# A feed-forward up projection by seven block products in place of eight, on one Trainium2 core

## The chip, the cores and the metric

The kernel runs on one core of one Trainium2 chip. The metric is the device time of one execution in microseconds. Of the kernel before, three runs were timed (891.97, 891.04 and 891.0 us, median 891.04), and one more execution was profiled.

## What is computed

`x` is 4 x 512 x 512 in fp32. Two layers are added to it. The first is a gated layer with its weights given per batch (`gate_up` 512 x 512, `ctx` 512 x 256), both matmuls in int8 with smoothed scales. The second is a mixture of experts with two experts chosen for all tokens together:

```python
x = x + xattn(layernorm(x), fside, ctx)          # 4 batches, int8 products
h = layernorm(x).reshape(-1, 512)                # 2048 tokens
logits = h @ gate_w.T
_, sel = top_k(logits.sum(axis=0), 2)            # two of eight experts, for all tokens
rw = softmax(logits[:, sel], axis=1)
u = gelu(einsum('nd,kdf->knf', h, w1[sel]) + b1[sel])   # up: 512 -> 2048
y = einsum('knf,kfd->knd', u, w2[sel]) + b2[sel]        # down: 2048 -> 512
x = x + einsum('nk,knd->nd', rw, y)
```

## The kernel before, in words

The program is written by engine: each of the five engines has a block with its instructions in the order written, and counting semaphores join them. PSUM has eight banks, in four slots of two.

**Attention part** (0 to about 147 us). The four batches pass through moments, normalisation, transposes on TensorE, the smoothing scale, rounding, the product, the gate and a second product. The use of the slots is a hand-written table (`SLOT_USES`, L74), and the calls stand by hand in an order that mixes the batches. At its end each batch is normalised again (`normalise`, `moments` with c = 2), transposed into slots `y.b.h` (`normed2`, L494), and split into a high part in fp32r (`keep_hi`, ScalarE, L741) and a low part (`keep_lo`, VectorE, L981, from PSUM and the high part): `xt_hi` and `xt_lo`. GpSimd adds the residual (`add_residual`, L326). The router (L504) multiplies the split x with the split gate weights; ScalarE sums the logits over tokens (L745), VectorE chooses two experts (`choose_experts`, L988 to L993) and picks their logits (`pick_logits`, L997 to L1008), GpSimd raises e to them (`lexp`, L378).

**Feed-forward part.** Every fp32 product is made as three fp32r products: high x high, high x low, low x high. The hidden dimension of the two experts is 32 column tiles of 128, in 8 groups of `FT` = 4. SP loads the raw weights of a tile (`load_unit`, 2 x 256 KB), ScalarE makes their high parts, VectorE the low parts. There are two sets of split weights, so a group's weights are made during the group before. For each group and each batch, PE alternates an up tile and the down tile of the hidden tile before it:

```python
for k in range(KD):                                # up, L624: 4 x 3 matmuls
    for a, v in ((w1_hi, xt_hi), (w1_hi, xt_lo), (w1_lo, xt_hi)):
        last = t.matmul(up_bank[f % 2][:, :], a[h][:, f, k, :], v[:, k, ds(at, T)], ...)
```

ScalarE reads the up bank twice: GELU in fp32 (`hid`, L853) and in fp32r (`h_hi`, L855). VectorE subtracts them (`h_lo`, L1120). A down tile (L638) is 4 token tiles x 3 matmuls into four y banks that accumulate over the 4 column tiles of a group; then VectorE multiplies by the router weight and adds to `res` (L1146). b1's rows of the two experts are loaded after the choice and transposed on PE (L665), b2 is added with the router weight by VectorE in the last group (L1137). SP stores each batch of `res` when it is done.

## Time and profile before

| | |
|---|---|
| median of 3 runs | 891.04 us |
| profiled execution, time | 887.1 us |
| profiled execution, span | 885.3 us |
| PE busy | 825.6 us, 93%, 3767 matmuls |
| PE weight load busy | 661.9 us, 75% |
| VectorE, ScalarE, GpSimd busy | 373.9, 307.9, 102.8 us |
| granted TensorE clock, mean | 0.975 |
| DMA | 32.29 MB, 36 GB/s over the span |

The time of an execution is its span and about 2 us around it. Busy time of an engine is the sum over its instructions, with overlaps counted once. Matmuls are pipelined: an instruction's recorded duration is longer than the distance to the next one, so what a stream of matmuls costs is read from the starts. PEld is the load of the stationary operand, which overlaps the matmul before it. `<-` behind an idle time names what ended it. POOL is GpSimd, DVE is VectorE, ACT is ScalarE.

### The profile page before, as it was taken

What the parts mean: (1) busy time and instruction counts of PE and PEld (TensorE: products, weight loads), DVE (VectorE), ACT (ScalarE), POOL (GpSimd) and SP (SyncE); (2) the same over time, 40 slices, a digit from 0 to 9 for tenths busy, and PEclk for the clock granted to TensorE, in tenths of its full rate; (3) what the DMA queues carried; (4) which work ended last, traced back from release to release, by engine and by line L of the source; (5) the groups of instructions that cost most, each with busy time, mean ns of one, the idle gap of its engine ahead of it and who ended that gap; (6) DMA issues with size and microseconds to landing.
All of it is one profiled execution on the core that took longest, in us unless ns stands there. A gap on an engine that the chain in (4) does not pass through costs nothing.

```text
span 885.3 us, 11147 instructions
## 1 busy us (share of the span) xinstructions
PE 825.6 (93%) x3767; PEld 661.9 (75%) x3767; DVE 373.9 (42%) x575; ACT 307.9 (35%) x532; POOL 102.8 (12%) x132
## 2 busy tenths in 40 slices
PE   3687877699999999999999999999999999999998
PEld 3565644388888888888888888888888888888886
DVE  2999997423333332333333323333333333334444
ACT  7975666422222222222222222222222222222221
POOL 1578884200000000000000000000000000000000
PEclk9798997899999999999999999999999999999999
DMA  9300000430000000000000000000000000000112
GB/s 347 129 1 1 1 1 0 144 96 24 24 24 25 24 24 24 24 24 24 24 24 24 24 24 24 24 24 24 24 24 24 24 1 0 0 1 1 47 47 95
DMA packets 27701, 32.29 MB, mean 36 GB/s; under 512 B 1400, under 2 KB 19864, under 8 KB 26784
## 3 DMA queue, kind: packets, MB, share of 16 engines
q1 hardware_dynamic: 27680, 32.02, 10.6%
q8 instruction: 12, 0.20, 0.1%
q14 instruction: 9, 0.07, 0.0%
HBM read 27.82 MB, written 4.19 MB: 36 GB/s over the span
## 4 chain that ended last, share of the span: by engine, by line
PE 82%; DVE 12%; DMA 2%; issue 1%; ACT 1%; SPq 1%; ACTq 0%; DVEq 0%
PE slot L638 40%; PE slot L624 39%; DVE rmax L910 3%; DVE peak_x L910 2%; DVE xv L960 2%; DMA wv<-in_fside_BxS2xS 2%; DVE stats L901 1%; DVE xv L973 1%; DVE wv L973 1%; PE slot L504 1%; DVE peak_a L910 1%; DVE scale L951 1%; DMA raw<-in_L_ffn_w 0%; PE slot L494 0%; DVE xt_lo L981 0%
## 5 line engine op out<-in xcount | busy, mean ns | idle before, releaser
L853 ACT ACTIVATE hid<-slot,b_col 128x512 f32<-128x512 f32 x128 | 88.0, 688 | 512.1 <-PE slot L624 511.6
L1120 DVE TENSOR_TENSOR h_lo<-hid,h_hi 128x512 fp32r<-128x512 f32 x128 | 88.4, 691 | 321.2 <-ACT h_hi L855 320.1
L624 PE MATMUL slot<-xt_hi,w_hi 128*128 (+1 forms) x512 | 203.1, 397 | 4.3 <-DVE w_lo L1012 4.3
L638 PE MATMUL slot<-w_hi,h_hi 128*128 128x512 f32 x512 | 203.5, 397 | 3.0 <-DVE h_lo L1120 3.0
L638 PE MATMUL slot<-w_hi,h_lo 128*128 128x512 f32 x512 | 201.9, 394 | 0.0
L624 PE MATMUL slot<-xt_hi,w_lo 128*128 (+1 forms) x512 | 201.4, 393 | 0.0
L624 PE MATMUL slot<-xt_lo,w_hi 128*128 (+1 forms) x512 | 200.5, 392 | 0.0
L638 PE MATMUL slot<-w_lo,h_hi 128*128 128x512 f32 x512 | 199.8, 390 | 0.0
L1146 DVE SCALAR_TENSOR_TENSOR res<-slot,rw,res 128x512 f32 x128 | 90.3, 751 | 139.0 <-PE slot L638 139.0
L624 PEld LDWEIGHTS slot<-xt_hi,w_hi 128*128 128x128 f32 x512 | 96.6, 189 | 25.1 <-DVE w_lo L1012 4.3
L638 PEld LDWEIGHTS slot<-w_hi,h_hi 128*128 128x128 f32 x512 | 96.4, 188 | 23.8 <-DVE h_lo L1120 3.4
L638 PEld LDWEIGHTS slot<-w_hi,h_lo 128*128 128x128 f32 x512 | 96.3, 188 | 23.6
L624 PEld LDWEIGHTS slot<-xt_hi,w_lo 128*128 128x128 f32 x512 | 96.5, 188 | 23.1
L638 PEld LDWEIGHTS slot<-w_lo,h_hi 128*128 128x128 f32 x512 | 96.6, 189 | 22.6
L624 PEld LDWEIGHTS slot<-xt_lo,w_hi 128*128 128x128 f32 x512 | 96.6, 189 | 21.5
L855 ACT ACTIVATE h_hi<-slot,b_col 128x512 fp32r<-128x512 f32 x128 | 86.9, 679 | 0.0
L476 PE MATMUL slot<-wq,xq 128*128 128x512 bf16 x96 | 22.6, 379 | 3.7 <-ACT wq L727 1.3
L679 ACT ACTIVATE xv<-res,nmr,rstd 128x512 f32<-128x512 f32 x32 | 23.2, 802 | 5.3 <-POOL nmr L294 5.3
L1126 DVE TENSOR_TENSOR w_lo<-raw,w_hi x28 | 19.4, 692 | 13.3 <-ACT w_hi L863 13.3
L910 DVE TENSOR_REDUCE peak_x<-slot 128x2 f32<-128x1024 f32 x16 | 19.0, 1213 | 13.6 <-PE slot L409 12.3
L1137 DVE SCALAR_TENSOR_TENSOR res<-b_row,rw,res 128x512 f32 x32 | 21.9, 746 | 0.0
L306 POOL TENSOR_TENSOR wv<-wv,xq 128x512 f32<-128x512 f32 x16 | 19.9, 1279 | 5.3 <-ACT xq L711 5.3
(117 smaller groups left out, 555.9 us busy)
## 6 DMA issues: line engine op xcount, KB each, us to landing
raw<-in_L_ffn_w SPq DMA_DIRECT2D x64, 256.0 KB, 2.8
res<-in_x SPq DMA_DIRECT2D x4, 1024.0 KB, 9.3
wv<-in_fside_BxS2xS SPq DMA_DIRECT2D x4, 1024.0 KB, 15.0
out_x<-res SPq DMA_DIRECT2D x3, 1024.0 KB, 3.9
cv<-in_ctx SPq DMA_DIRECT2D x4, 512.0 KB, 11.4
out_x<-res SPq DMA_DIRECT2D x4, 256.0 KB, 2.7
b_row<-in_L_ffn_b SPq DMA_DIRECT2D x2, 256.0 KB, 4.4
b_rows<-in_L_ffn_b SPq DMA_DIRECT2D x2, 8.0 KB, 2.6
```

The source lines that it names most:

```text
L306: g.tensor_tensor(w[:, j, :], w[:, j, :], rows[b][:, 0:n], ALU.mult).then_inc(wmul_ready[b], 1)
L476: last = t.matmul(ps[:, j, :], xq[b][:, k, at:at + P], wq[b][:, k, :], start=(k == 0), stop=(k == n - 1))
L624: last = t.matmul(up_bank[f % 2][:, :], a[h][:, f, k, :], v[:, k, ds(at, T)], start=(n == 0), stop=(n == 3 * KD - 1))
L638: last = t.matmul(y_bank[j][:, :], a[f % 2][:, j * P:(j + 1) * P], v[h][:, f, :], start=(f == 0 and n == 0), stop=(f == FT - 1 and n == 2) ...
L679: s.activation(xv[b][:, j, :], res[:, b * TT + j, :], ACT.Identity, bias=nmr[c - 1][b][:, j:j + 1], scale=rstd[c - 1][b][:, j:j + 1]).then ...
L853: s.activation(hid[f % 2][:, :], up_bank[f % 2][:, :], ACT.Gelu_apprx_tanh, bias=bias).then_inc(hid_ready, 1)
L855: s.activation(h_hi[f % 2][:, :], up_bank[f % 2][:, :], ACT.Gelu_apprx_tanh, bias=bias).then_inc(hid_ready, 1)
L910: return v.tensor_reduce(dst, src, AX.X, ALU.max, apply_absolute_value=True)
L1120: v.tensor_tensor(h_lo[f % 2][:, :], hid[f % 2][:, :], h_hi[f % 2][:, :].bitcast(F32), ALU.subtract).then_inc(h_ready, 1)
L1126: v.tensor_tensor(w1_lo[nxt][:, ds(b, 1)], raw1[:, ds(b, 1)], w1_hi[nxt][:, ds(b, 1)].bitcast(F32), ALU.subtract).then_inc(w_ready, 1)
L1137: ins = v.scalar_tensor_tensor(out=r, in0=b2_row[:, k, :], scalar=rw[:, k * (PAIRS // TOPK), ds(b * TT + j, 1)], in1=r, op0=ALU.mult, op1= ...
L1146: ins = v.scalar_tensor_tensor(out=r, in0=y_bank[j][:, :], scalar=rw[:, p, ds(b * TT + j, 1)] if final else rw[:, ds(p, 1), ds(b * TT + j, ...
```

## The change

The up projection is now done on 2 x 2 blocks. The blocks of x are (depth half h) x (batch of a pair), those of w1 are (column tile f of a pair) x (depth half), named A11, A12, A21, A22. Seven products of blocks replace eight (the Winograd form of Strassen's scheme): with S1 = A21 + A22, S2 = S1 - A11, S3 = A11 - A21, S4 = A12 - S2 on the weight side and T1 to T4 on the side of x. Each operand is split in a high and a low part as before, so a product of blocks is 2 depth tiles x 3 = 6 matmuls of 128x512.

What moves:

- **Tiles.** 16 pairs of column tiles (`PAIRS`), and within each two pairs of batches (`tp`). PE makes seven products (`strassen`) in banks `x_bank`, `p_bank`, `w_bank`, then four down tiles from them. Up and down tiles no longer alternate.
- **x.** 14 operands of 128 x 2 x 512 per pair of batches (`xo`, and `xf` in fp32 over the same memory) in place of `xt_hi`, `xt_lo`. ScalarE keeps a full and a high copy of each block (`keep_block`), GpSimd makes T1 to T4 (`operand_sums`), ScalarE their high parts (`operand_hi`), VectorE their low parts (`operand_lo`). VectorE's low parts of batches 0 to 2 (`keep_lo`) read the full copy in SBUF, not PSUM. The working tiles of the attention part (`xv`, `xq`, `wq`, `rows`) now lie over the same memory. The order of some calls at the end of the attention part changes.
- **Weights.** One set of split operands of seven each (`a_hi`, `a_lo`), refilled during the second half of a pair: ScalarE casts operand i when product i is done, GpSimd sums (`weight_sums`) and makes the low parts. For the first pair VectorE makes sums and low parts.
- **Hidden tiles.** After product 0 ScalarE copies `x_bank` to `e1`; VectorE makes five combinations (`combine`, PSUM + SBUF) into `e1`, `e2`, `e3`; ScalarE makes GELU twice for each of four hidden tiles; GpSimd makes their low parts (`hid_lo`), which was VectorE's.
- **b1** of all experts is loaded with the inputs, transposed at the start, and the two chosen rows are picked by VectorE (`pick_bias`). **b2** is added one token tile per pair in the loop. **Loads** of w1 and w2 are 512 KB each, one of each per pair.

The diff, cut to its core:

```diff
-    FT = 4
-    GROUPS = DFF // (FT * P)
-    PAIRS = TOPK * GROUPS // 2
+    FW = 2 * P
+    EP = DFF // FW
+    PAIRS = TOPK * EP
...
             sp.dma_start(gw_rows, gate_w).then_inc(gw_load, 16)
+            sp.dma_start(b1_rows[:, :], b1_v).then_inc(b1_load, 16)
...
+            def operand_sums(tp, router_use):
+                even, odd = 2 * tp, 2 * tp + 1
+                slot_i, n = place(router_use)
+                kept(even, 0)
+                kept(odd, 0)
+                pool.wait_ge(filled[slot_i], n + 1)
+                g.tensor_tensor(part(tp, T1L), part(tp, T1H), part(tp, T2H), ALU.subtract).then_inc(tsum_ready[tp], 1)
+                kept(odd, 1)
+                pool.wait_ge(tsum_ready[tp], 1)
+                g.tensor_tensor(part(tp, T2L), part(tp, T3H), part(tp, T1L), ALU.subtract).then_inc(tsum_ready[tp], 1)
+                g.tensor_tensor(part(tp, T3L), part(tp, T3H), part(tp, T1H), ALU.subtract).then_inc(tsum_ready[tp], 1)
+                kept(even, 1)
+                pool.wait_ge(tsum_ready[tp], 2)
+                g.tensor_tensor(part(tp, T4L), part(tp, T4H), part(tp, T2L), ALU.subtract).then_inc(tsum_ready[tp], 1)
+
+            operand_sums(0, "r.1")
+            operand_sums(1, "r.3")
...
+            def pair(p, final):
+                for i in range(4):
+                    hid_lo(p, 0, i)
+                if not final:
+                    weight_sums(p)
+                    weight_lo(p, 0)
+                hid_lo(p, 1, 0)
+                if not final:
+                    weight_lo(p, 1)
+                    weight_lo(p, 2)
+                hid_lo(p, 1, 1)
+                hid_lo(p, 1, 2)
+                hid_lo(p, 1, 3)
+                if not final:
+                    weight_lo(p, 3)
...
+            def pair(p, first, final):
+                for tp in range(2):
+                    q = 2 * p + tp
+                    pe.wait_ge(hid_ready, 8 * q + 2)
+                    strassen(p, tp, 0, x_bank, True, first)
+                    pe.wait_ge(comb_ready, 5 * q + 4)
+                    strassen(p, tp, 1, p_bank, True, first)
+                    pe.wait_ge(e1_ready, q + 1)
+                    strassen(p, tp, 2, x_bank, False, first)
+                    pe.wait_ge(comb_ready, 5 + 5 * q + 1)
+                    strassen(p, tp, 3, p_bank, False, first)
+                    pe.wait_ge(comb_ready, 5 * q + 5)
+                    strassen(p, tp, 4, w_bank, True, first)
+                    pe.wait_ge(comb_ready, 5 + 5 * q + 2)
+                    strassen(p, tp, 5, p_bank, False, first)
+                    pe.wait_ge(comb_ready, 5 + 5 * q + 3)
+                    strassen(p, tp, 6, w_bank, False, first)
+                    if tp == 0:
+                        pe.wait_ge(w2_ready, 2 * p + 2)
+                    down(p, tp, 0, 0, 0, True)
+                    down(p, tp, 0, 2, 1, False)
+                    last = down(p, tp, 1, 1, 1, True)
+                    if tp == 1 and not final:
+                        last.then_inc(w2_free, 1)
+                    down(p, tp, 1, 3, 0, False)
...
+            def keep_block(b, h):
+                ps, empty = drain(f"y.{b}.{h}")
+                s.copy(xo[b // 2][:, HI_AT[b % 2][h], :, :], ps[:, :, :])
+                s.copy(part(b // 2, FULL_AT[b % 2][h]), ps[:, :, :].rearrange("p k t -> p (k t)")).then_inc(empty, 1)
...
             keep_lo(1, 0)
+            keep_lo(1, 1)
             moments(3, 2)
-            keep_lo(1, 1)
             keep_lo(2, 0)
             keep_lo(2, 1)
-            keep_lo(3, 0)
-            keep_lo(3, 1)
+            last_lo(3, 0)
+            last_lo(3, 1)
             choose_experts()
...
             pick_logits()
-            split_lo(0)
...
+            operand_lo(0, 0)
+            pick_bias()
+            first_weights()
```

**How the order changes, place 1: VectorE from the choice of the experts to the first weight part.** Before (`lk`, `lsub`: picked logits; `w_lo`: low parts of w1 and w2):

```order
L999 TENSOR_SCALAR onehot<-iota,top_f 128x8 [waits dve_link] x2
L1003 TENSOR_TENSOR picked<-slot,onehot 128x128 [waits logcol_ps,dve_link]
L1005 TENSOR_REDUCE lk<-picked 128x16 [waits dve_link]
L1003 TENSOR_TENSOR picked<-slot,onehot 128x128 [waits dve_link]
L1005 TENSOR_REDUCE lk<-picked 128x16 [waits dve_link]
L1006 TENSOR_TENSOR lmax<-lk 128x16 [waits dve_link]
L1008 TENSOR_TENSOR lsub<-lk,lmax 128x16 [waits dve_link]
L1008 TENSOR_TENSOR lsub<-lk,lmax 128x16
L1012 TENSOR_TENSOR w_lo<-raw,w_hi 128x512 [waits w_hi_ready]
```

and now, behind the same operations (`xo<-xf,xo` is an operand's low part, `b_all` is b1 of all experts, `a_lo` a weight operand's low part, `ssum` a weight sum):

```order
L1191 TENSOR_TENSOR lsub<-lk,lmax 128x16
L1165 TENSOR_TENSOR xo<-xf,xo 128x1024 [waits thi_ready0,tsum_ready0]
L1196 TENSOR_TENSOR picked<-b_all,onehot 128x128
L1198 TENSOR_REDUCE b_col<-picked 128x16 [waits dve_link]
L1196 TENSOR_TENSOR picked<-b_all,onehot 128x128 [waits dve_link]
L1198 TENSOR_REDUCE b_col<-picked 128x16 [waits dve_link]
L1203 TENSOR_TENSOR a_lo<-raw,a_hi 128x256 [waits dve_link,a_hi_ready,raw1_load]
L1207 TENSOR_TENSOR ssum<-raw 128x256
L1207 TENSOR_TENSOR ssum<-ssum,raw 128x256 [waits sums_ready]
```

Five operations now stand between the logits and the first weight part, and behind it sums, further weight parts and three more operand parts.

**Place 2: GpSimd at the same time.** Before, lexp followed at once on the last normalisation scales (`rstd`, `nmr`). Now:

```order
L320 TENSOR_TENSOR nmr_3<-nmean_3,rstd_3 128x4 [waits rstd_ready3]
L413 TENSOR_TENSOR xf<-xf 128x1024 [waits filled2,drained1]
L416 TENSOR_TENSOR xf<-xf 128x1024 [waits tsum_ready0,drained0]
L417 TENSOR_TENSOR xf<-xf 128x1024
L420 TENSOR_TENSOR xf<-xf 128x1024 [waits tsum_ready0,drained3]
L413 TENSOR_TENSOR xf<-xf 128x1024 [waits filled0,drained3,drained1]
L416 TENSOR_TENSOR xf<-xf 128x1024 [waits tsum_ready1,drained2]
L417 TENSOR_TENSOR xf<-xf 128x1024
L420 TENSOR_TENSOR xf<-xf 128x1024 [waits tsum_ready1,drained0]
L426 TENSOR_TENSOR lexp<-euler,lsub 128x32 [waits lsub_ready]
```

Eight operations on 1024 elements stand ahead of lexp; the fifth waits for the last router product (`filled0`).

**Place 3: PE in the loop of the feed-forward part.** Before, the end of a down tile and the up tile and down tile that follow:

```order
L638 MATMUL slot<-w_hi,h_lo 128x512
L620 ISA
L624 MATMUL slot<-xt_hi,w_hi 128x512 [waits w_ready]
L624 MATMUL slot<-xt_lo,w_hi 128x512
L624 MATMUL slot<-xt_hi,w_lo 128x512
...
L630 REGISTER_ALU
L638 MATMUL slot<-w_hi,h_hi 128x512 [waits h_ready,w_ready]
```

and now products 2 and 3 of a half:

```order
L719 REGISTER_ALU [waits e1_ready]
L726 MATMUL slot<-xo,a_hi 128x512 [waits a_ops_ready]
L726 MATMUL slot<-xo,a_hi 128x512
L726 MATMUL slot<-xo,a_lo 128x512
L726 MATMUL slot<-xo,a_hi 128x512 x2
L726 MATMUL slot<-xo,a_lo 128x512
L756 REGISTER_ALU
L719 REGISTER_ALU [waits comb_ready]
L726 MATMUL slot<-xo,a_hi 128x512 [waits a_ops_ready]
```

PE now waits every 6 matmuls for another engine's reading of a bank that was filled one product earlier, where it waited every 12 for a hidden tile that was 12 matmuls old.

## Rows read from the trace of the kernel before

**Rows 1.** The page: busy times, chain that ended last, w1/w2 loads

```profile
PE 825.6 (93%) x3767; PEld 661.9 (75%) x3767; DVE 373.9 (42%) x575; ACT 307.9 (35%) x532; POOL 102.8 (12%) x132
...
PE 82%; DVE 12%; DMA 2%; issue 1%; ACT 1%; SPq 1%; ACTq 0%; DVEq 0%
...
raw<-in_L_ffn_w SPq DMA_DIRECT2D x64, 256.0 KB, 2.8
```

**Rows 2.** Busy time by engine from 300 to 500 us

```profile
core 0: us, PE busy (x) PEld busy (x) DVE busy (x) ACT busy (x) POOL busy (x), PEclk, DMA share, GB/s
300.00:500.00 200.00, 200.00 (x870) 162.80 (x869) 61.47 (x90) 55.22 (x91) 0.00 (x0) 1.00 0.08 25
```

**Rows 3.** Waits: us in total, times, longest us

```profile
ACT hid L853 <- PE slot L624: 511.6, 126, 6.9
```

**Rows 4.** Timeline of the steady state: start us, us, engine, instruction

```profile
333.27 0.40 PE L638 MATMUL slot<-w_hi,h_hi 128*128 128x512 f32 x1
...
333.57 0.69 ACT L853 ACTIVATE hid<-slot,b_col 128x512 f32<-128x512 f32 x1 [4.27 <-PE slot L624]
...
334.15 0.68 ACT L855 ACTIVATE h_hi<-slot,b_col 128x512 fp32r<-128x512 f32 x1
...
336.04 0.40 PE L624 MATMUL slot<-xt_hi,w_hi 128*128 128x512 f32 x1
```

**Rows 5.** Timeline from the last router matmul to the first weight parts

```profile
158.50 0.40 PE L504 MATMUL slot<-xt_hi,gwt_lo 128*8 128x512 f32 x1
...
163.86 5.43 POOL L378 TENSOR_TENSOR lexp<-euler,lsub 128x32 f32<-128x32 f32 x1 [17.52 <-DVE lsub L1008]
...
165.42 0.69 DVE L1012 TENSOR_TENSOR w_lo<-raw,w_hi 128x512 fp32r<-128x512 f32 x1 [1.64 <-ACT w_hi L750]
...
166.17 0.80 PE L624 MATMUL slot<-xt_hi,w_hi 128*128 128x512 f32 x1 [4.26 <-DVE w_lo L1012]
...
168.57 0.69 DVE L1015 TENSOR_TENSOR w_lo<-raw,w_hi 128x512 fp32r<-128x512 f32 x1
```

**Rows 6.** Timeline around the gap ahead of the first down tile

```profile
173.55 0.39 PE L624 MATMUL slot<-xt_hi,w_lo 128*128 x1
...
176.90 0.79 PE L638 MATMUL slot<-w_hi,h_hi 128*128 128x512 f32 x1 [2.96 <-DVE h_lo L1120]
```

**Rows 7.** Chain of waits at the end: start us, us, what

```profile
879.83 1.37 PE slot L638 x6
```

**Rows 8.** Timeline of SP's queue at the start

```profile
0.73 0.41 SPq L209 DMA_DIRECT2D wsc_row<-in_L_ffn_gate_w  x1
```

**Rows 9.** Groups by line and form: count, busy us, mean ns

```profile
L1146 DVE SCALAR_TENSOR_TENSOR res<-slot,rw,res 128x512 f32 x128 | 90.3, 751 | 139.0 <-PE slot L638 139.0
L306 POOL TENSOR_TENSOR wv<-wv,xq 128x512 f32<-128x512 f32 x16 | 19.9, 1279 | 5.3 <-ACT xq L711 5.3
L318 POOL TENSOR_TENSOR xv<-xv 128x256 f32<-128x256 f32 x16 | 11.2, 732 | 0.5 <-ACT xv L737 0.5
L973 DVE SCALAR_TENSOR_TENSOR wv<-slot,scale,wsc_row 128x512 f32<-128x512 f32 x16 | 11.1, 741 | 0.0
L981 DVE TENSOR_TENSOR xt_lo<-slot,xt_hi 128x1024 fp32r<-128x1024 f32 x8 | 9.5, 1216 | 5.0 <-ACT xt_hi L741 5.0
L741 ACT CAST xt_hi<-slot 128x1024 fp32r<-128x1024 f32 x8 | 7.8, 1006 | 2.3 <-PE slot L494 2.3
```

**Rows 10.** Timeline: GpSimd's residual adds and short VectorE operations beside them

```profile
102.13 2.51 POOL L326 TENSOR_TENSOR res<-res,wv 128x512 f32<-128x512 f32 x2
103.67 0.98 DVE L927 TENSOR_TENSOR ratio<-clip,crec 128x2 f32<-128x2 f32 x1
...
118.02 0.20 DVE L927 TENSOR_TENSOR ratio<-clip,crec 128x2 f32<-128x2 f32 x1
...
137.03 3.73 POOL L326 TENSOR_TENSOR res<-res,wv 128x512 f32<-128x512 f32 x3
138.78 0.78 DVE L906 TENSOR_SCALAR nmean<-mv 128x4 f32<-128x4 f32 x1
139.48 1.31 DVE L907 TENSOR_SCALAR var_e<-mv 128x4 f32<-128x4 f32 x1
```

More of the change, by code:

```diff
@@ L672, in _ @@
+            pair(0, True, False)
+            with pe.Fori(1, PAIRS - 1) as p:
+                pair(p, False, False)
+            pair(PAIRS - 1, False, True)
         @block.scalar
@@ L870, in _ @@
+            pair(0, True, False)
+            with act.Fori(1, PAIRS - 1) as p:
+                pair(p, False, False)
+            pair(PAIRS - 1, False, True)
         @block.vector
@@ new lines, in _, with token_weights @@
+            operand_lo(0, 0)
+            pick_bias()
+            first_weights()
+            def token_weights():
+                dve.wait_ge(lexp_ready, 1)
+                link(v.tensor_tensor(lden[:, :], lexp[:, 0, :], lexp[:, 1, :], ALU.add))
+                link(v.reciprocal(lrec[:, :], lden[:, :]))
+                for k in range(TOPK):
+                    ins = v.tensor_tensor(rw[:, k * EP:(k + 1) * EP, :], lexp[:, k:k + 1, :].to_broadcast([P, EP, NT]),
+                                          lrec[:, :].unsqueeze(1).to_broadcast([P, EP, NT]), ALU.mult)
+                link(ins)
```

536 lines of the change are left out of this document (331 added, 205 removed), and 6 rows, old and new, of the table SLOT_USES.

## The prediction

> **What bounds the kernel now.** I read the page first, then the stretches by engine, the waits, and the timelines of the steady state, of the entry into the feed-forward part and of the end. TensorE is busy 93% of the span, and the chain that ended last is PE for 82% [rows 1]. Between 300 and 500 us it is busy for all 200.00 us at a granted clock of 1.00, the 2.4 GHz level [rows 2]. The long waits are those of ScalarE and VectorE for PE, 511.6 us the longest [rows 3]. So this part costs what its matmuls cost. Their cadence: the first matmul of a down tile starts at 333.27, the first of the next up tile, 12 matmuls on, at 336.04 [rows 4]: 2.768 us for 12, 0.2306 us each (the recorded 0.39 us of each overlaps the next); 870 in 200 us [rows 2] says the same. 3072 matmuls give 708.4 us. The first starts at 166.17, after a wait of 4.26 [rows 5], and the last ends at 879.83 + 1.37 = 881.2 [rows 7]: 715.0 us. So the entry loses 6.6 us, mostly by the gap between the last up matmul, 173.55, and 176.90 [rows 6] and by matmuls at the lower clock (0.80 us for the first one [rows 5]). 166.2 us lie ahead of the part, 4.1 behind.
>
> **What the change removes.** 128 up tiles of 12 matmuls are 1536. A pair of column tiles and a pair of batches now take seven products of 6 matmuls in place of eight: 32 x 42 = 1344. The down matmuls stay at 1536. 192 x 0.2306 = **-44.3 us**, all on the path. The change does what it says: the order has 42 + 48 matmuls per half of a pair.
>
> **Start.** b1's load stands ahead of x and w on SP; one issue there takes 0.41 us [rows 8], and the path begins with those loads: **+0.4** (0 if the next loads are not late by it, 0.9 if PE's transpose matters too).
>
> **The end of the attention part.** The new operands need a high and a full copy: ScalarE makes 2 more copies of 128x1024 for each batch, 1.01 us each [rows 9], and VectorE's low parts of batches 0 to 2, 1.2 us each [rows 9], now read two SBUF tensors. The last router product ended near 158.9 [rows 5]. (1) Batch 0's copies hold back VectorE's next link by 1.1 us, and batch 1's second low part moves ahead of batch 3's moments, 1.2 us on VectorE: 2.5 with the waits. (2) Batch 2's two extra copies stand ahead of batch 3's high parts on ScalarE: 2.0. (3) Router 1 leaves its place ahead of batch 3's transposes: -1.7. (4) GpSimd's operand sums for batches 0 and 1 run here and meet VectorE's two-input operations. What that does is in the trace. The 128x2 ratio takes 0.20 us at 118.02 and 0.98 at 103.67, ending at 104.65, just as GpSimd's adds end (102.13 + 2.51); var_e takes 1.31 and ends with the adds from 137.03, and nmean before it ends at 139.56, between two adds of that run [rows 10]. So VectorE gets its turn between two GpSimd instructions. A GpSimd subtraction or product of two tensors takes 0.73 us for 256 elements and 1.28 for 512 [rows 9], so about 2.4 for 1024. Two low parts, each held for part of one: 1.6. Sum **+4.4** (1.5 if the copies find slack, 7 if each meeting costs all of 2.4).
>
> **From the choice to the first matmul.** The first load is now 512 KB in place of 256; I add 0.9 us to the 2.8 of the page's loads [rows 1]. Meanwhile GpSimd begins the second set of sums when the last router product ends, about 163.3: four of 2.4 us, to 173.3 with VectorE's turns. VectorE's queue here has onehot, lmax, lsub, the low part of T2 (1.1 us), b1's choice (1.2) and the first weight part (0.4), nearly all with two SBUF inputs, one per GpSimd instruction. So most of it runs after 173.3, for 3.5 us: first matmul at 176.9, 10.7 later than before, of which 4.4 is counted. **+6.3**; 0.9 if VectorE gets through, 9 if the sums stretch.
>
> The Trainium skill (SBUF — State Buffer, SBUF: two separate sides) says that a GpSimd operation and a VectorE operation with two SBUF inputs exclude each other for the whole instruction. By it, lexp would hold VectorE too, and the sum would be 5.4 more (a rival below). For lexp the trace does not agree: GpSimd has it from 163.86 for 5.43 us, and the low parts from 165.42 to 168.57, four of them, run inside it at 0.69 each [rows 5]; for GpSimd's adds it agrees.
>
> **Inside the entry.** Before its first combination VectorE makes seven weight parts, four chained sums and three operand parts; I get that combination at 184.3, where PE could use it at 181. Products then run from 176.9 to 190.7, 4.1 us beyond 42 x 0.2306; 0.7 for hidden tile 2 behind GpSimd and 1.0 for matmuls at the lower clock make 5.8 for the 6.6 of before, **-0.8** (-4 to +5).
>
> **Steady state.** With product 0 of a half starting at t = 0, product k ends at 1.38(k+1). A reader starts 0.30 us after the next matmul starts (333.27, 333.57) [rows 4]. VectorE reads the bank of product 1 (0.69 us, a little over half of the 1.22 for 1024 [rows 9]) while PE runs product 2: release at 0.30 + 0.69 + 0.05 = 1.04 of 1.38, and of the rest 0.2 goes to the weight load that must precede the matmul and 0.1 to register work. It just fits; the same holds behind products 3 and 4. So the handoffs cost **0** (96 of them, up to 0.2 each). The hidden tiles: product 4 is combined by 7.9; GELU 1 runs 8.0 to 9.3 (two activations, 333.57 to 334.15 + 0.68 [rows 4]); in a half that also refills the weights a cast (0.35) is next; GELU 2 ends at 10.8, GpSimd's low part (1.25) at 12.1, and PE wants it at 12.45 less 0.2. At 10.8 VectorE also comes to the b2 adds, which have two SBUF inputs and take 0.75 like the y adds [rows 9]: if it is first, GpSimd ends at 12.85 and PE stalls 0.7, if second not at all. I take half, 16 x 0.35 = **+5.6** (0 to 11). GpSimd's whole load per pair, 8 x 1.25 + 11 x 0.7 + 2 x 1.25 = 20 of 41.5 us, and VectorE's 21 fit. Weight loads are issued a pair ahead and stay hidden. The tail is as before.
>
> **Sum:** -44.3 + 0.4 + 4.4 + 6.3 - 0.8 + 5.6 = -28.4. The profiled execution took 887.1 us (span 885.3), so 858.7. The median of the runs, 891.04, is 0.4% above the profiled one; scaled by that, **862 us**.
>
> **The rivals.**
> *Cheap entry.* VectorE gets its turns, and the b2 adds miss GpSimd: -44.3 + 0.4 + 5 - 0.8 = -39.7, 851 us. For it: the ratio at 118.02 shows no stretch in a part where GpSimd is mostly busy [rows 10]. Against it: var_e's 1.31.
> *Late handoffs.* Register work and weight load don't fit into what is left of 1.38 us, and each of 96 handoffs costs 0.15: +14.4, 877 us (867 at 0.05, 881 at 0.2). For it: my slack is 0.04 us. Against it: no row shows a loss, but no handoff of before was this tight.
> *lexp holds VectorE.* If VectorE's weight parts wait behind the sums and then for the 5.43 us of lexp as well: 862 + 5.4, 868 us. The rows speak against it, low parts ran at 0.69 inside lexp [rows 5]. It is what the rule of the Trainium skill quoted above would give.
> *Slower: GpSimd paces the down tiles.* It now makes all low parts of hidden tiles, beside VectorE's combinations and adds, which read PSUM and one SBUF tensor. If these exclude GpSimd too, parts 1 and 2 start behind a combination each, and PE waits 1.2 us in each of 32 halves: +38, 901 us. It decides from 28.4 / 32 = 0.9 us per half. Against it: the dequantisation (PSUM and one SBUF tensor) takes 0.74 us in a part where GpSimd is mostly busy, and the same operation 0.75 with GpSimd idle [rows 9].
>
> **How the numbers follow.** Forecast 0.45 (856 to 869), cheap entry 0.25, late handoffs 0.17, lexp 0.05, GpSimd pacing 0.08. From 850 to 879 the range holds nearly all of the first, two thirds of the second, most of the third, and lexp: 0.8. Within 0.2%, about what a measurement can tell, there is almost nothing: faster 0.91, same 0.01, slower 0.08.
>
> **What would show it.** Right: 2880 matmuls of 128x512 in the part at 0.23 us cadence; the first at 174 to 179; a PE wait of some tenths once per pair ahead of the second down tile; VectorE operations between 162 and 174 stretched to the ends of GpSimd's. Wrong: gaps between the products of a half (late handoffs); a PE wait ahead of a down tile in every half (pacing); a first matmul before 172 (cheap entry); a granted clock under 1.00 in the steady state.

## The result, and the profile after

Against the kernel before in the same comparison (891.48 us, median of 4 runs, 891.0 to 891.97), the changed kernel takes **849.0 us** (median of 4, 847.23 to 850.53): ratio 0.952, 95% interval 0.950 to 0.955. The forecast of 862 had the right sign and missed by 13 us; the result lies 1 us below the range's low end.

Rows of the page of the changed kernel (profiled execution 847.2 us), which answer to [rows 1]:

```profile
span 845.4 us, 11484 instructions
PE 772.4 (91%) x3569; PEld 620.1 (73%) x3575; DVE 487.1 (58%) x695; ACT 365.1 (43%) x675; POOL 458.6 (54%) x463
...
PE 78%; DVE 14%; issue 3%; POOL 2%; ACT 2%; DMA 2%; SPq 0%; DVEq 0%; POOLq 0%; ACTq 0%
...
raw<-in_L_ffn_w SPq DMA_DIRECT2D x32, 512.0 KB, 3.3
```

PE has 192 weight loads fewer (3767 before, 3575 now), one for each matmul forecast; its matmul records are 198 fewer, but six of the int8 products' 96 are missing from this profile. GpSimd works 459 us in place of 103. PE still ends last. The stretch from 300 to 500 us of the changed kernel, in the columns of [rows 2]:

```profile
300.00:500.00 200.00, 200.00 (x879) 164.45 (x879) 97.86 (x137) 69.77 (x131) 102.47 (x102) 1.00 0.08 26
```

This is the surprise. PE is as full as in [rows 2] and at the same granted clock of 1.00, yet 879 matmuls fall into the 200 us and not 870. The timeline shows it product by product (first matmul of a half's seven products, first of its down products):

```profile
287.45 0.62 PE L726 MATMUL slot<-xo,a_hi 128*128 128x512 f32 x2
...
296.97 0.39 PE L739 MATMUL slot<-w_hi,h_hi 128*128 128x512 f32 x1
```

42 matmuls take 9.52 us: **0.2267 us each, not 0.2306**. The six handoffs inside those 9.52 us cost nothing, as forecast (in the first half of a pair the same 42 take up to 9.57). The down products take 10.88 us for 48 (0.2267 again) in the first half of a pair and 11.1 in the second, where one wait stands:

```profile
257.20 3.18 POOL L431 TENSOR_TENSOR h_lo<-e,h_hi 128x512 fp32r<-128x512 f32 x2 [0.23 <-ACT e L984]
...
257.67 1.55 DVE L1363 SCALAR_TENSOR_TENSOR res<-b_row,rw,res 128x512 f32 x1 [0.16 <-DVE res L1363]
...
258.72 0.19 PEld L739 LDWEIGHTS slot<-w_hi,h_hi 128*128 128x128 f32 x1 [0.32 <-POOL h_lo L431]
```

The b2 addition (1.55 us, alone 0.75) and GpSimd's low parts (3.18 for two, alone 2.6) stretch each other; TensorE's weight load waits 0.32 us for the second, and the stream of matmuls loses 0.2.

The entry, from the timeline of the changed kernel (answers to [rows 5]):

```profile
158.33 3.35 POOL L420 TENSOR_TENSOR xf<-xf 128x1024 f32<-128x1024 f32 x1
...
159.38 3.38 DVE L1151 TENSOR_TENSOR xo<-xf,xo 128x1024 fp32r<-128x1024 f32 x1
...
168.12 0.15 DVE L1171 TENSOR_REDUCE logit_sum<-logit_part 8x1 f32<-8x4 f32 x1 [3.09 <-ACT wsc_row L867]
...
169.85 2.49 DVE L1182 TENSOR_SCALAR onehot<-iota,top_f 128x8 f32<-128x8 f32 x2
169.93 2.37 POOL L416 TENSOR_TENSOR xf<-xf 128x1024 f32<-128x1024 f32 x1
...
174.08 0.39 ACT L871 CAST a_hi<-raw 128x256 fp32r<-128x256 f32 x1
...
174.68 2.35 DVE L1191 TENSOR_TENSOR lsub<-lk,lmax 128x16 f32<-128x16 f32 x2
...
177.10 6.34 POOL L426 TENSOR_TENSOR lexp<-euler,lsub 128x32 f32<-128x32 f32 x1 [0.20 <-DVE lsub L1191]
178.09 0.35 DVE L1196 TENSOR_TENSOR picked<-b_all,onehot 128x128 f32<-128x128 f32 x1
...
180.27 1.19 PE L726 MATMUL slot<-xo,a_hi 128*128 128x512 f32 x2 [9.87 <-DVE a_lo L1203]
```

Two 128x8 operations take 2.49 us and two 128x16 ones 2.35, as long as the GpSimd subtraction beside them: of each two, one is short (0.23, 0.16) and one lasts to the subtraction's end, so VectorE gets its turn once per subtraction. Inside the pow (177.10, 6.34 us) a two-input operation takes 0.35. The first matmul starts at 180.27, 14.1 later than in [rows 5].

### The profile page after: what moved, and what is told of

It reads as the page before. It is cut to its first block, busy times and chain, and to the rows that moved or that the text cites. A ratio compares the mean times of both kernels' runs of the same rounds, so it can differ in the third digit from the quotient of the medians.

```text
span 845.4 us, 11484 instructions
## 1 busy us (share of the span) xinstructions
PE 772.4 (91%) x3569; PEld 620.1 (73%) x3575; DVE 487.1 (58%) x695; ACT 365.1 (43%) x675; POOL 458.6 (54%) x463
## 4 chain that ended last, share of the span: by engine, by line
PE 78%; DVE 14%; issue 3%; POOL 2%; ACT 2%; DMA 2%; SPq 0%; DVEq 0%; POOLq 0%; ACTq 0%
PE slot L739 41%; PE slot L726 35%; DVE rmax L1080 3%; DVE peak_x L1080 2%; DVE xf L1130 2%; DMA wv<-in_fside_BxS2xS 2%; DVE xo L1151 1%; DVE stats L1071 1%; DVE wv L1143 1%; DVE xf L1143 1%; DVE scale L1121 1%; DVE peak_a L1080 1%; POOL h_lo L431 1%; PE slot L603 1%; PE slot L524 0%
## 5 line engine op out<-in xcount | busy, mean ns | idle before, releaser
L726 PE MATMUL slot<-xo,a_hi 128*128 128x512 f32 x896 | 277.7, 391 | 11.5 <-DVE a_lo L1203 9.9
L1371 DVE SCALAR_TENSOR_TENSOR res<-slot,rw,res 128x512 f32<-128x512 f32 x256 | 178.6, 751 | 136.5 <-PE slot L739 136.5
L1336 DVE TENSOR_TENSOR e<-slot,e 128x512 f32<-128x512 f32 x160 | 110.6, 691 | 183.2 <-PE slot L726 183.2
L726 PEld LDWEIGHTS slot<-xo,a_hi 128*128 128x128 f32 x896 | 168.4, 189 | 47.8 <-issue 9.9
L726 PE MATMUL slot<-xo,a_lo 128*128 128x512 f32 x448 | 174.9, 390 | 0.0
L431 POOL TENSOR_TENSOR h_lo<-e,h_hi 128x512 fp32r<-128x512 f32 x96 | 135.6, 1425 | 58.4 <-ACT e L984 57.3
L726 PEld LDWEIGHTS slot<-xo,a_lo 128*128 128x128 f32 x448 | 84.5, 189 | 17.8
L983 ACT ACTIVATE h_hi<-e,b_now 128x512 fp32r<-128x512 f32 x96 | 69.2, 721 | 64.3 <-DVE e L1336 63.9
L984 ACT ACTIVATE e<-e,b_now 128x512 f32<-128x512 f32 x96 | 68.0, 708 | 0.0
L450 POOL TENSOR_TENSOR w_lo<-raw,w_hi 128x512 fp32r<-128x512 f32 x30 | 38.7, 1290 | 51.9 <-ACT w_hi L874 51.9
L445 POOL TENSOR_TENSOR a_lo<-ssum,a_hi 128x256 fp32r<-128x256 f32 x60 | 44.0, 745 | 0.0
```

The source lines that it names most:

```text
L431: g.tensor_tensor(h_lo[:, i, :], hid[i][:, :], h_hi[:, i, :].bitcast(F32), ALU.subtract).then_inc(h_ready, 1)
L445: g.tensor_tensor(a_lo[:, i, :, :], A_OF[i], a_hi[:, i, :, :].bitcast(F32), ALU.subtract).then_inc(a_ops_ready, 1)
L450: g.tensor_tensor(w2_lo[:, f, :], raw2[:, f, :], w2_hi[:, f, :].bitcast(F32), ALU.subtract).then_inc(w2_ready, 1)
L726: last = t.matmul(dst, a[:, i, k, :], xo[tp][:, v, k, :], start=(start and n == 0), stop=(n == 3 * H - 1), skip_group_check=True)
L983: s.activation(h_hi[:, i, :], src, ACT.Gelu_apprx_tanh, bias=bias).then_inc(hid_ready, 1)
L984: s.activation(hid[i][:, :], src, ACT.Gelu_apprx_tanh, bias=bias).then_inc(hid_ready, 1)
```

## The experiments

Four questions: what sets the 0.2267; what the entry waits for; whether b1's place matters; what the wait in the down products is. "Spare tile" below is an SBUF tile that nothing uses.

**1. All tiles 32 bytes higher, both kernels.** In both, ahead of `res`:

```
+        pad = sb("pad", [P, 8])
```

> The kernel before with an unused tile of 32 bytes a partition allocated ahead of res, so that every operand of a matmul starts 32 bytes higher in SBUF: at an odd multiple of 32 bytes, as in the changed kernel, where it was a multiple of 64. No instruction changes. Theory A (the place of the operands in SBUF sets whether a matmul of 512 columns takes 0.2306 or 0.2267 us): 12 matmuls go from 2.765 to about 2.72 us, the FFN part (3072 matmuls) shortens by 10 to 12 us, 879 to 882 us against 891. Theory B (the order of the matmuls or the traffic of the other engines sets it): 12 matmuls stay at 2.765 us and the time within 0.2% of 891.

Measured 890.99 us (888.96 to 893.18; ratio to before 0.999, 0.997 to 1.002); 12 matmuls still take 2.763 and 2.77 us.

> The changed kernel with the same unused tile of 32 bytes ahead of res, so that its operands start at multiples of 64 bytes, as in the kernel before. Theory A (place in SBUF): the 42 matmuls of seven products go from 9.53 to 9.69 us, the FFN part lengthens by about 10 us, 857 to 861 us against 849. Theory B (order or traffic): 9.53 us stays, 849 us within 0.4%.

Measured 848.24 us; the 42 matmuls still take 9.53. Whether operands start at a multiple of 64 bytes is not it. Theory B, order or traffic, seemed to be left.

**2. The matmul by itself.** Behind the last matmul of each kernel, with all else done:

```
+            for r in range(8):
+                t_up1(bank[r % 2])
+            for r in range(8):
+                t_up2(bank[r % 2])
+                t_down2()
+            for r in range(8):
+                pe.wait_ge(gw_load, 16)
+                pe.wait_ge(consts_ready, 1)
+                t_up3(bank[r % 2])
...
+            for r in range(8):
+                t_down4()
```

> The kernel before with 480 further matmuls of 512 columns behind its last one, when all other engines have done and no transfer but the last stores runs; they write PSUM only and nothing reads them. First 96 in groups of 12 as an up product, one behind the other; then 8 times 12 of an up product and 12 of a down product without any wait; then the same 8 times with two waits, long met, ahead of each 12; then 96 of down products. Theory A (the two kinds of product taking turns every 12 matmuls costs): the first and the last stretch run at 0.2267 us a matmul, as in the changed kernel, the second and third at 0.2306. Theory B (the waits ahead of every 12): only the third at 0.2306. Theory C (the other engines' traffic): all four at 0.2267 or below. Theory D (the tiles' places, in a way that a shift of all by 32 bytes does not touch): all four at about 0.2306.

> The changed kernel with the same 480 matmuls behind its last one, on its own operands and in the same four stretches. Theory A (taking turns): 0.2267, 0.2306, 0.2306, 0.2267 us a matmul. Theory B (waits ahead of every 12): 0.2267, 0.2267, 0.2306, 0.2267. Theory C (traffic) and theory D (places): 0.2267 or below in all four.

(They are 576 matmuls; the 480 of these texts was miscounted.) In the changed kernel every stretch runs at 0.2266 (the first at 0.2282, its first matmuls included). In the kernel before, the timeline of these matmuls gives these rows: the 13th and the last matmul of the first stretch (up products alone); the starts of twelve downs, of the twelve ups behind them and of the next downs in the second stretch; the first and the last matmul of the last stretch (down products alone).

```profile
890.15 0.39 PE L679 MATMUL slot<-xt_hi,w_hi 128*128 128x512 f32 x1
...
909.14 0.39 PE L679 MATMUL slot<-xt_hi,w_lo 128*128 128x512 f32 x1
...
923.16 0.40 PE L688 MATMUL slot<-w_hi,h_hi 128*128 128x512 f32 x1
...
925.93 0.40 PE L683 MATMUL slot<-xt_hi,w_hi 128*128 128x512 f32 x1
...
928.70 0.40 PE L688 MATMUL slot<-w_hi,h_hi 128*128 128x512 f32 x1
...
997.87 0.39 PE L702 MATMUL slot<-w_hi,h_hi 128*128 128x512 f32 x1
...
1019.40 0.39 PE L702 MATMUL slot<-w_hi,h_lo 128*128 128x512 f32 x1
```

Down products alone: 21.53 / 95 = 0.2266. Up products alone: 18.99 / 83 = 0.2288, and every twelve of them in 2.747 us, 0.2289. In turn, both kinds: 2.77 for twelve, 0.2307, with waits or without. All this with the other engines idle. So neither traffic nor waits nor the order as such (with the changed kernel's operands the turns run at 0.2266); it comes with the up product's operands of the kernel before.

**3. Which operand.** Six stretches of 96 behind the kernel before:

```
+                        t.matmul(dst, W[n][:, 0, k, :], V[n][:, k, :], start=(k + n == 0), stop=(k + n == 5))
+                        t.matmul(dst, HS[n][:, k * P:(k + 1) * P], X[n][:, k, 0:T], start=(k + n == 0), stop=(k + n == 5))
...
```

> The kernel before with six stretches of 96 further matmuls of 512 columns behind its last, nothing else running, each in groups of 12 to one of two banks: (1) the up product's weights against w2's rows as moving operand; (2) the hidden state as weights against xt as moving operand; (3) the up product with xt's first row for all four depths; (4) with four slices of xt that lie 2048 bytes apart rather than 8192; (5) with one block of weights for all four depths, xt as in the up product; (6) the up product's high parts alone. Theory A (xt as moving operand, wherever it is read): 2, 3, 4, 5 and 6 at 0.230 us a matmul, 1 at 0.2267. Theory B (its depths 8192 bytes apart, as nothing in the changed kernel is): 2, 5 and 6 at 0.230, 1, 3 and 4 at 0.2267. Theory C (the tiles of w1's parts as weights): 1, 3, 4, 5 and 6 at 0.230, 2 at 0.2267. Theory D (only the pair of the two, or the switch between high and low parts): all but one or two at 0.2267.

w1 as weights against w2 takes 2.72 us for twelve, 0.2267; the five stretches with xt as moving operand take 2.747, 0.2289, whatever the depths, the weights or the parts. The last of them, as one row of the timeline:

```profile
994.57 22.14 PE L705 MATMUL slot<-xt_hi,w_hi 128*128 128x512 f32 x96
```

(22.14 less the last one's 0.39, over 95, is 0.2289.) Theory A. But the changed kernel's moving operands lie behind `res` in SBUF too, and there they cost nothing. What is left is where the two operands stand to each other. By the programs' allocation, xt's rows start 128 bytes behind a multiple of 512, the parts of w1 and w2 and the hidden states 320 behind one; in the changed kernel all start 96 behind one. xt is the only moving operand that doesn't match its weights.

**4. Match it in the kernel before, spoil it in the changed one.** In both, ahead of `raw1`:

```
+        pad = sb("pad", [P, 80])
```

> The kernel before with an unused tile of 320 bytes a partition between xt_lo and raw1, so that all weights and the hidden states start 1152 bytes into a block of 2048 bytes, as xt does, where they started 832 bytes in. No instruction changes. Theory A (a matmul is slower where its moving operand and its weights start at different places of such a block; xt against w1 or the hidden state was so, w2 against either was not, and nothing in the changed kernel is): all groups of 12 matmuls go from 2.763 and 2.77 to 2.72 us, and the time falls by 256 times 0.045, 11 to 12 us, to 880. Theory B (the place is not it: xt's reads are slower wherever the weights lie): 2.765 stays, 891 us within 0.3%.

Measured **880.27 us** (878.07 to 882.12), ratio to before 0.987 (0.985 to 0.989). Windows and timeline of that kernel:

```profile
300.00:500.00 200.00, 200.00 (x884) 165.60 (x883) 63.17 (x93) 56.94 (x94) 0.00 (x0) 1.00 0.07 24
```

```profile
500.70 0.39 PE L639 MATMUL slot<-w_hi,h_hi 128*128 128x512 f32 x1
...
503.42 0.39 PE L625 MATMUL slot<-xt_hi,w_hi 128*128 x1
```

884 matmuls in place of 870 [rows 2], 2.72 us for twelve. A spare tile of 320 bytes, with no instruction changed, makes the kernel before 11 us faster.

> The changed kernel with the same unused tile of 320 bytes between its operands of the seven products and raw1: the weights start 416 bytes into a block of 2048, the products' moving operands 96. Theory A: the seven products go from 9.53 to 9.61 us or, if switching between the two kinds costs too, up to 9.69; 32 times 0.08 to 0.16 is 2.6 to 5 us, 852 to 854 us. Theory B: 9.53 us stays, 849 us within 0.2%.

Measured **859.13 us** (857.14 to 860.11), 10 us slower and twice what was expected. Windows, and the first of the seven products and of the down products:

```profile
300.00:500.00 200.00, 200.00 (x868) 162.12 (x867) 99.19 (x137) 71.11 (x133) 103.28 (x101) 1.00 0.08 26
```

```profile
291.13 0.63 PE L727 MATMUL slot<-xo,a_hi 128*128 128x512 f32 x2
...
300.93 0.39 PE L740 MATMUL slot<-w_hi,h_hi 128*128 128x512 f32 x1
```

42 matmuls in 9.80 us, 0.2333; 1344 x 0.0066 is 8.9 of the 10. Undone in one kernel and brought about in the other, the place moves the time both ways: it is the cause, and its price depends on the distance.

**5. The price by distance.** Behind the changed kernel, eleven times, c floats into the hidden state:

```
+            for r in range(4):
+                for j in (0, 1, 2, 0, 1, 2, 0, 1, 2, 0, 1, 2):
+                    t.matmul(bank[r], h_hi[:, 0, j * P + 8:(j + 1) * P + 8], w2_hi[:, 0, :], start=True, stop=True)
```

> The changed kernel with 528 matmuls of 512 columns behind its last one, nothing else running: eleven stretches of 48, w2's high part as moving operand, slices of the hidden state's high part as weights, which start 0, 32, 64, 128, 192, 256, 320, 384, 448, 480 and again 0 bytes behind the place (modulo 512) where the moving operand starts. Theory A (the two places modulo 512 must agree): 0.2267 us at 0 bytes, and 0.2285 to 0.2335 at all others, by a rule that the eleven values may show; 320 bytes gives the 0.2333 of the changed kernel with its weights shifted by 320, and 192 (what xt and w1 have in the kernel before) 0.229. Theory B (it is not the difference but the mixture of two kinds of place in turn): 0.2267 in all eleven stretches, as every matmul of a stretch has the same difference.

Its timeline, one row for each stretch of 48 after the first, in the order 32, 64, 128, 192, 256, 320, 384, 448, 480, 0 bytes:

```profile
855.26 11.35 PE L784 MATMUL slot<-w_hi,h_hi 128*128 128x512 f32 x48
866.45 11.36 PE L787 MATMUL slot<-w_hi,h_hi 128*128 128x512 f32 x48
877.65 11.32 PE L790 MATMUL slot<-w_hi,h_hi 128*128 128x512 f32 x48
888.81 11.16 PE L793 MATMUL slot<-w_hi,h_hi 128*128 128x512 f32 x48
899.81 11.06 PE L796 MATMUL slot<-w_hi,h_hi 128*128 128x512 f32 x48
910.71 11.36 PE L799 MATMUL slot<-w_hi,h_hi 128*128 128x512 f32 x48
921.90 11.32 PE L802 MATMUL slot<-w_hi,h_hi 128*128 128x512 f32 x48
933.06 11.16 PE L805 MATMUL slot<-w_hi,h_hi 128*128 128x512 f32 x48
944.06 11.36 PE L808 MATMUL slot<-w_hi,h_hi 128*128 128x512 f32 x48
955.25 11.04 PE L811 MATMUL slot<-w_hi,h_hi 128*128 128x512 f32 x48
```

From start to start over 48 (the last row: 11.04 less 0.39, over 47):

| weights behind moving, bytes | 0 | 32 | 64 | 128 | 192 | 256 | 320 | 384 | 448 | 480 |
|---|---|---|---|---|---|---|---|---|---|---|
| us a matmul | 0.2266 | 0.2331 | 0.2333 | 0.2325 | 0.2292 | 0.2271 | 0.2331 | 0.2325 | 0.2292 | 0.2331 |

192 (320 less 128, the kernel before's up product) gives its 0.229 and 320 the 0.2333 of experiment 4. Theory A, with one correction: 256 bytes cost next to nothing, so what counts is nearly the distance modulo 256. Why the distance matters inside the chip, no run here shows.

**6. GpSimd's differences behind the pow.**

```
             operand_sums(0, "r.1")
-            operand_sums(1, "r.3")
...
                             lsub[:, :, :].rearrange("p k n -> p (k n)"), ALU.pow).then_inc(lexp_ready, 1)
+            operand_sums(1, "r.3")
```

> The changed kernel with GpSimd's four differences for batches 2 and 3 issued behind the softmax's pow rather than ahead of it. Theory A (the choice of experts waits because VectorE's two-input operations and GpSimd's subtractions can't be under way at once): both onehot operations fall from 2.49 us to under 1, lmax from 0.98 to under 0.2, both lsub from 2.35 to under 0.2, the pow starts by 171 us and the first matmul of the FFN part by 176 us (held then by w1's landing and its cast at about 174), 4 to 5 us earlier than 180.27; part of this is given back where the differences now stretch VectorE's sums of weights and come late for batches 2 and 3: 843 to 849 us. Theory B (these operations wait for something else): the choice is as long as before, and the second pair of batches comes later, 849 to 856 us.

Measured 858.95 us (856.51 to 859.68), 10 slower. Both halves of theory A are right and its sum is wrong. From logit_sum to the first matmul 7.3 us pass in place of 12.15: without a subtraction beside them the same small operations are short. Then the differences meet VectorE's low parts of weights and operands, and product 3 waits 10.4 us for a combination that stands behind them in VectorE's queue. From the timeline:

```profile
173.96 0.50 DVE L1182 TENSOR_SCALAR onehot<-iota,top_f 128x8 f32<-128x8 f32 x2
...
176.22 0.26 DVE L1191 TENSOR_TENSOR lsub<-lk,lmax 128x16 f32<-128x16 f32 x2
...
185.68 3.40 DVE L1165 TENSOR_TENSOR xo<-xf,xo 128x1024 fp32r<-128x1024 f32 x1
...
197.23 1.22 PE L726 MATMUL slot<-xo,a_hi 128*128 128x512 f32 x2 [10.41 <-DVE e L1336]
```

**7. VectorE's choice in another order.** (The diff is cut, its places in the order of execution; `subtract_max` holds the steps lmax and lsub.)

```
             pick_logits()
-            operand_lo(0, 0)
-            pick_bias()
             first_weights()
...
                 weight_lo(0)
+                operand_lo(0, 0)
...
                 weight_lo(1)
+                pick_bias()
                 weight_lo(2)
+                subtract_max()
```

> The changed kernel with VectorE's steps of the choice in another order: after onehot and the two reductions it waits for w1 at once and makes the first product's low part; the choice of the biases and lmax and lsub, stretched to 1 and 2.4 us beside GpSimd's subtractions, come behind the sums of weights. Theory A (the first matmul waits for VectorE's queue and not for w1): it starts 3.5 to 4.5 us earlier behind the choice, within 1.5 us of the first cast of w1, and the time falls by 2 to 4 us, 845 to 847 us. Theory B (what is moved out of the way comes due within the entry, since GpSimd's pow and the biases then come late): the first matmul is as much earlier, but product 3 or the first down product waits for it, and the time stays at 849 us within 1.

Measured 851.89 us (849.98 to 852.89). The first matmul starts at 177.5, 9.2 us behind logit_sum in place of 12.15, but lsub moves to 182.70 and the pow to 183.04, ahead of every low part on GpSimd, and product 3 waits 3.63 us where it waited 1.60. Nothing is won; the time is 2.9 us longer, more than theory B allowed. That fits an entry bound by the sum of GpSimd's work and VectorE's, whichever of them waits first.

**8. b1 loaded last.** Its load behind c's, its transpose with the logits', its copy with the choice of biases.

```
-            sp.dma_start(b1_rows[:, :], b1_v).then_inc(b1_load, 16)
...
                 sp.dma_start(cv[b][:, :, :], cx_v[b]).then_inc(c_load[b], 16)
+            sp.dma_start(b1_rows[:, :], b1_v).then_inc(b1_load, 16)
```

> The changed kernel with b1 loaded behind all other inputs, its transpose issued just ahead of the logits' and its copy out of PSUM just ahead of the choice of the biases, so that the start is that of the kernel before. Theory A (the attention part's slip of 2.9 us by 100 us is the 0.45 to 0.71 us of the load at the start, and meetings of VectorE's and GpSimd's operations that the shift brings about): at 100 us the program stands within 0.5 us of the kernel before, and the time is 2 to 3 us shorter, 846 to 847. Theory B (the slip has another cause, such as the other places of the tiles): the start moves by 0.5 us, and at 100 us the slip is still over 2 us, 848.5 us.

Measured 849.73 us (849.1 to 851.27): no gain. The start itself is that of the kernel before again: VectorE's first maximum of x comes at 13.79 us, against 14.48 in the changed kernel and 13.89 before. But in this execution a later load landed late, the third maximum comes at 19.03 in place of 18.70, and the gain is gone. What makes the rest of the slip is told below, under "Own time and median": it comes without b1 too.

**9. The wait in the down products, three ways.** GpSimd's two low parts of weights behind those of the hidden states:

```
                 hid_lo(p, 1, 0)
-                if not final:
-                    weight_lo(p, 1)
-                    weight_lo(p, 2)
                 hid_lo(p, 1, 1)
...
+                    weight_lo(p, 1)
+                    weight_lo(p, 2)
```

> The changed kernel with GpSimd's low parts of the next pair's second and third products issued behind the four low parts of the hidden states rather than between the first and the second of them. Theory A (TensorE's wait of 0.2 to 0.3 us once per pair, in the down products of the second two batches, is for GpSimd's third low part): that wait goes, both runs of 48 down matmuls take 10.88 us, and the time falls by 15 times 0.2, 3 us, 846 us. Theory B (it is for VectorE, whose additions of b2 hold the PSUM banks): 11.1 us stays and the time is 849 us.

Measured 849.05 us (847.52 to 850.85), the wait unchanged (0.32 us, 11.08 us for the 48). ScalarE's cast behind the last gelu:

```
                     gelu(p, 1, 1, e3[:, :])
-                    next_hi(3)
...
-                    for i in (4, 5, 6):
+                    for i in (3, 4, 5, 6):
```

> The changed kernel with ScalarE's cast of the next pair's fourth product issued behind the last gelu of the second two batches, rather than between the second gelu and the third. Theory A (the wait of 0.2 to 0.33 us in the down products, once per pair, is for the third low part, which GpSimd begins when ScalarE's third hidden state is there; it is 0.39 us of this cast late): the wait goes, both runs of 48 down matmuls take 10.88 us, and the time falls by 3 us, to 846. Theory B (it is late because VectorE's second addition of b2, 1.55 us in place of 0.76, and GpSimd's subtraction hold each other up): the wait shrinks by less than half, and the time is within 1.5 us of 849.

Measured 851.36 us (849.98 to 853.17), 2.4 slower, and the wait is still there (11.12 us for the 48). VectorE's b2 additions behind four of the down products' additions:

```
+                        if tp == 1 and s == 1:
+                            dve.wait_ge(y_free, TT + NT * p + 3 * TT)
...
```

> The changed kernel with VectorE's two additions of b2 issued behind the first four additions of the down products' sums rather than ahead of them, away from GpSimd's low parts of the hidden states. Theory A (the wait in the down products is the cast on ScalarE): it stays at 0.2 us a pair. Theory B (VectorE's additions of b2 and GpSimd's low parts hold each other up, which is what the prediction priced at 0.35 us a pair): the two low parts under way then fall from 3.18 to 2.6 us, the wait goes, both runs of 48 take 10.88 us, 846 us.

Measured **845.94 us** (844.75 to 846.68), ratio to before 0.949 (0.947 to 0.951), the fastest of all. The same pair of low parts, and one b2 addition, in that kernel's timeline:

```profile
259.12 2.55 POOL L431 TENSOR_TENSOR h_lo<-e,h_hi 128x512 fp32r<-128x512 f32 x2 [0.23 <-ACT e L984]
...
264.57 0.75 DVE L1364 SCALAR_TENSOR_TENSOR res<-b_row,rw,res 128x512 f32 x1 [0.17 <-DVE res L1371]
```

3.18 has become 2.55 and 1.55 has become 0.75; 883 matmuls fall into the 200 us, and 48 down matmuls take 10.90 on the average. Theory B, and 849.0 - 845.9 = 3.1 us is its price; in the profiles, first to last matmul of the part take 658.1 us in place of 660.8, 2.7 of it.

**10. The same with the first differences held back** until VectorE has batch 2's low parts:

```
+            pool.wait_ge(lo_ready[2], 2)
             operand_sums(0, "r.1")
```

> The changed kernel with the additions of b2 late, as in the run that measured 845.94, and with GpSimd's first four differences held back until VectorE has made both low parts of batch 2. Theory A (these low parts, 6.1 us for two of 1.22, wait for GpSimd's differences, and the last two router products wait for them): the low parts take 2.4 us, the choice comes 3 to 3.7 us earlier, and as GpSimd then works without a gap until 178 us, 1 to 2 us of that stay: 844 to 845 us. Theory B (GpSimd's 19 us of differences bound the entry, since they only move): the choice is earlier, the weights' sums are stretched instead, and the time is 845.9 within 1, or up to 847 as GpSimd ends a microsecond later.

Measured 848.21 us (846.66 to 849.55), 2.3 slower than experiment 9's. Each low part takes 1.23 again and the choice is earlier, but GpSimd, whose eight subtractions now follow one another until 179.6, stretches all that VectorE does meanwhile, and the first matmul comes at 182.81. Theory B, and by more than it said.

## Why the prediction was wrong, by its own steps

**Removed matmuls, and the step that failed.** 192 fewer, the count is right. But the cadence of 0.2306 us, read from [rows 4] with its count in [rows 2], was taken as what a matmul of 512 columns costs, for the 192 and silently for the other 2880. It was what one costs with xt and w1 at the distance they have in the kernel before. The new tiles happen to remove that distance: 2880 x 0.0039 = **11.2 us**, in no term and in no rival. Of it the up products' own price is 1536 x 0.0022 = 3.4; the rest comes with the two kinds taking turns (0.2289 and 0.2266 alone, 0.2307 in turn), and matching the places removes that too (experiment 4). The same tiles 320 bytes off would have hidden most of it (859.13).

The Trainium skill ("SBUF — State Buffer", "Who interferes with whom") gives TensorE two SBUF read ports, one for the moving operand and one for the weight load, and calls them independent. Taken by itself, that rule leaves no room for the distance to matter. Experiments 4 and 5 don't agree: 0.2266 against 0.2333.

**Steady state.** The handoffs cost 0, as forecast. The meeting of the b2 additions with GpSimd's low parts happens once per pair, at the place the text named; its size was off: forecast 16 x 0.35 = 5.6, measured 3.1 (experiment 9). Half of a 0.7 worst case was a guess between two orders; in fact the order repeats, and costs 0.2 each time.

**Entry.** Forecast against measured, with landmarks that stand in every trace. VectorE's last reciprocal of the attention part comes at 131.14 in the changed kernel, and in experiment 1's execution of the kernel before at:

```profile
131.21 0.18 DVE L953 RECIPROCAL rscale<-scale 128x4 f32<-128x4 f32 x1
...
164.43 0.15 DVE L989 TENSOR_REDUCE logit_sum<-logit_part 8x1 f32<-8x4 f32 x1 [3.94 <-ACT wsc_row L746]
...
170.81 0.80 PE L625 MATMUL slot<-xt_hi,w_hi 128*128 128x512 f32 x1 [4.22 <-DVE w_lo L1013]
```

From there to logit_sum 33.2 us before and 37.0 after: **+3.8** for the end of the attention part (forecast 4.4). This term rests on one execution of each; over the profiles of all runs that leave this stretch as it is, it takes 32.5 to 33.3 us in the kernel before and 36.9 to 38.7 in the changed one, on the average 4.5 more. From logit_sum to the first matmul 6.4 and 12.15: **+5.8** (forecast 6.3). From the first matmul's start to the last one's the changed kernel takes 841.05 - 180.27 = 660.8 us; less 2879 x 0.2267 and the 3.1, 5.0 are lost; the kernel before with matched operands (experiment 4) loses 6.5 by the same count: **-1.5** (forecast -0.8). The pow didn't hold VectorE. The first matmul came at 180.27, where 176.9 was forecast and 174 to 179 given as the sign of being right; it is late by the 4 us that are told below, under "Own time and median". The parts of the sum that called for GpSimd and VectorE to exclude each other held to within a microsecond.

That a GpSimd operation and a VectorE operation with two SBUF inputs exclude each other is what the Trainium skill states ("SBUF — State Buffer", "SBUF: two separate sides"), for the whole instruction. The trace agrees for GpSimd's subtractions against lmax, lsub, the low parts and the b2 additions; for the pow it does not (0.35 us at 178.09, inside 6.34). VectorE's short operations of one SBUF tensor and a scalar are held up in the same way (onehot, 2.22 us for the second of the two at 169.85).

**The sum again**, from the kernel before with matched operands (880.27): 192 x 0.2267 = -43.5, +3.8, +5.8, -1.5, +3.1, and 0.5 for b1 (forecast 0.4; VectorE's first operation comes 0.43 later in the profiled execution, its first maximum 0.59) make -31.8; 849.0 - 880.3 = -31.3. With 4.5 in place of 3.8 it would be -31.1. So of the 42 us between the two kernels 11 are the tiles' place, and 31 the change.

**The rivals.** Late handoffs, lexp and GpSimd pacing didn't happen: no gap between products, no wait in every half. "Cheap entry" would give 851, close to the result, but for the wrong reason: the entry was as dear as forecast.

**Own time and median.** The forecast was scaled by 0.4% because the profiled execution of before was faster than the median. That was right, and here is where it comes from: VectorE's scale from its maxima, beside GpSimd's products and halves, in the kernel before, and in experiment 1's execution of it:

```profile
63.33 0.44 DVE L951 TENSOR_SCALAR scale<-rmax 128x4 f32<-128x4 f32 x1
63.71 1.41 POOL L318 TENSOR_TENSOR xv<-xv 128x256 f32<-128x256 f32 x2
```

```profile
63.59 1.82 DVE L952 TENSOR_SCALAR scale<-rmax 128x4 f32<-128x4 f32 x1
63.97 1.41 POOL L319 TENSOR_TENSOR xv<-xv 128x256 f32<-128x256 f32 x2
```

The same operation takes 0.44 us in the one and 1.82 in the other, where it ends with GpSimd's two instructions (63.97 + 1.41); it got its turn ahead of them or only behind them, though in both executions it started 0.38 us before they did. Compared instruction by instruction, VectorE's queue falls behind in seven steps of 0.4 to 1.4 us, four of them at this scale, gains 0.5 twice, and the last reciprocal comes at 127.29 in the one and 131.21 in the other. The changed kernel's profile (131.14) was of the second kind. So 4 of the 14.1 us by which its first matmul was later are a difference that two executions of the kernel before show as well. Over the profiles of all runs this reciprocal comes between 127.3 and 133.5 in the kernel before (five profiles) and between 131.1 and 134.5 in the changed one (twelve), so whether the change adds a microsecond here besides b1 stays open.

## What to carry to other kernels

Before a cadence is carried over to a changed kernel, ask what it is made of: where moving operand and weights lie to each other modulo 256 bytes is part of it, and moving or resizing a tile between them changes it. Laying both out at the same place modulo 512 costs some spare bytes and was worth 1.3% here, 11 of the 42 us. And where GpSimd subtracts tensors, count VectorE's operations with two SBUF inputs, and its short tensor_scalar ones, as one per GpSimd instruction, put them where GpSimd is idle (b2: 3.1 us), and don't expect that moving GpSimd's work to another time helps while the sum of both bounds the stretch (experiments 6, 7, 10).

## What the runs showed of the hardware that was not expected

- A matmul of 128x128 by 512 fp32r columns, each with its own weight load, takes 0.2266 us where weights and moving operand start at the same place modulo 512 bytes, 0.2271 at 256 bytes' distance, up to 0.2333 elsewhere; a shift of both together does nothing (experiment 1: 2.763 and 2.77 us for twelve, and 9.53 for 42, as without it).
- Where two kinds take turns every 12, one at 0.2289 and one at 0.2266 alone, both run at 0.2307. Why the mixture is slower than either isn't explained by any run here, and stays open.
- GpSimd's pow of 128x32 (5.43 us in the kernel before, 6.34 in the changed one) stretches none of VectorE's two-input operations inside it, unlike its subtractions. But it may be held up itself: it takes 5.43 us in all five profiles of the kernel before, where VectorE's next such operation comes 1.5 us after its start, and 6.34 to 6.40 in all twelve of the changed one, where VectorE is in the middle of an operand's low part as it starts (176.95 to 178.16 beside 177.10). That it waits for that low part is inferred from the times; no run of the changed kernel took the low part away.
